# A fused four-layer decoder: wide attention's first maxima and last exponentials for two heads at once, and the feedforward's products behind the maxima of layer 2

## The reference, cut to what matters

```python
# layer 2, both attentions: 16 heads of width 8, softmax over 256 keys
# layer 2, feedforward (batches one by one)
h = layernorm(x, ln1_w, ln1_b); h = bitlinear(h, w1, b1)     # 128 -> 512, int8 activations, ternary weights
h = gelu(h); h = layernorm(h, ln2_w, ln2_b); x = x + bitlinear(h, w2, b2)
# layer 3, self-attention ("wide": 16 heads of width 64)
q, k, v = x @ Wq + bq, x @ Wk + bk, x @ Wv + bv
prob = softmax(k_h . q_h / 8);  out = sum(prob * v);  x = x + concat(out) @ Wo + bo
# layer 3, attention between the 16 heads of one token ("cross" below)
energy = einsum('nhld,ngld->nlhg', q, k); attn = softmax(energy / sqrt(128), axis=3)
out = layernorm(einsum('nlhg,ngld->nhld', attn, v)); x = x + out @ Wo.T + bo
# then layer 3's feedforward, which needs all batches
```

## Time and profile before

| | us |
|---|---|
| time, median of 3 runs | 1146.28 (1145.36 to 1150.3) |
| the profiled execution: device time | 1154.05 |
| the profiled execution: span from first to last instruction | 1152.2 |
| PE busy in the span | 854.2 (74%) |
| DVE busy | 605.4 (53%) |
| ACT busy | 358.4 (31%) |
| POOL busy | 317.2 (28%) |
| mean granted clock of PE | 0.849 |

### The profile page before, as it was taken

How to read it: one execution, slowest core, us unless ns; L and a number is a source line. 1 busy time by engine, 2 the same in 40 slices (tenths; PEclk the granted TensorE clock), 3 DMA queues, 4 the chain that set the end, 5 groups by cost and what they waited for, 6 DMA issues and landing times. The chain is left out here.

```text
span 1152.2 us, 16025 instructions
## 1 busy us (share of the span) xinstructions
PE 854.2 (74%) x5977; PEld 613.6 (53%) x5977; DVE 605.4 (53%) x1422; ACT 358.4 (31%) x697; POOL 317.2 (28%) x319
## 2 busy tenths in 40 slices
PE   5965887854676175688776757999999997367984
PEld 2532454553343173567653335576877775244884
DVE  2655852314499933585666886435236456642222
ACT  1110574220121112055544633453432332111331
POOL 1353100212168704132221111000034343415222
PEclk9975898985678597599988878899999997658998
DMA  9302200540000007053561000000000000005674
GB/s 374 118 1 81 69 5 1 164 131 7 19 0 1 0 1 165 10 116 65 139 179 52 3 1 0 1 2 2 2 1 2 1 2 1 0 1 189 194 262 154
DMA packets 44678, 72.44 MB, mean 63 GB/s; under 512 B 4817, under 2 KB 36737, under 8 KB 43033
## 3 DMA queue, kind: packets, MB, share of 16 engines
q1 hardware_dynamic: 38921, 65.72, 19.4%
q0 software_dynamic: 1728, 3.59, 0.9%
q10 hardware_dynamic: 3952, 2.10, 0.7%
HBM read 58.65 MB, written 15.89 MB: 65 GB/s over the span
## 5 line engine op out<-in xcount | busy, mean ns | idle before, releaser
L848 DVE TENSOR_REDUCE space<-PS 128x2 f32<-128x512 f32 x128 | 83.5, 686 | 42.6 <-PE PS L652 42.1
L2517 DVE TENSOR_REDUCE space<-PS 128x2 f32<-128x512 f32 x64 | 44.3, 692 | 114.3 <-PE PS L2221 114.3
L832 ACT ACTIVATE annex<-PS 128x384 f32<-128x384 f32 (+1 forms) x128 | 67.4, 545 | 59.7 <-PE PS L663 30.2
L2237 PE MATMUL PS<-space 64*128 64x256 f32 x256 | 80.4, 407 | 0.0
L2256 PEld LDWEIGHTS PS<-space 128*128 128x128 f32 x512 | 62.4, 192 | 23.0 <-issue 19.4
L2256 PE MATMUL PS<-space 128*128 128x65 f32 x512 | 71.1, 282 | 2.6 <-ACT space L2344 2.6
L1951 POOL TENSOR_TENSOR space<-space 128x1536 f32<-128x1536 f32 x16 | 54.6, 3439 | 39.1 <-ACT space L1824 32.9
L1171 PE MATMUL PS<-space 128*128 128x128 f32 x444 | 55.6, 278 | 9.3 <-DVE space L1306 5.4
L2344 ACT ACTIVATE space<-PS 128x512 f32<-128x512 f32 x64 | 38.2, 597 | 74.1 <-PE PS L2238 74.1
L1171 PEld LDWEIGHTS PS<-space 128*128 128x128 f32 x444 | 51.7, 192 | 12.3 <-DVE space L1306 6.5
L1306 DVE TENSOR_TENSOR space<-PS,space 128x512 f32<-128x512 f32 (+1 forms) x28 | 19.2, 687 | 71.6 <-ACT space L1233 66.4
(11 more groups left out here) (494 smaller groups left out, 2259.8 us busy)
## 6 DMA issues: line engine op xcount, KB each, us to landing
space<-in_e_l_ffn SPq DMA_DIRECT2D x22, 768.0 KB
space<-in_e_l_ffn SPq DMA_DIRECT2D x23, 192.0 KB, 2.7
l_ffn_sorted<-in_slots SPq DMA_DIRECT2D x2, 1584.0 KB, 25.9
space<-l_attn_scratch_k SPq DMA_DIRECT2D x8, 384.0 KB
space<-l_ffn_sorted SPq DMA_DIRECT2D x10, 264.0 KB, 4.4
weights<-in_w_l_xattn SPq DMA_DIRECT2D x1, 2504.0 KB, 15.3
weights<-in_w_l_attn SPq DMA_DIRECT2D x1, 2124.0 KB, 12.1
space<-l_xattn_scratch_q SPq DMA_DIRECT2D x4, 512.0 KB, 3.5
```

The costliest lines, as they stand in the source:

```text
L832: nc.scalar.activation(P[:, u % 8, 0:keys], PS[:, 3 + u % 2, 0:keys], ACT.Exp).then_inc(exp_done, 1)
L848: nc.vector.tensor_reduce(m[:, :, at_h], max_bank(u).rearrange("p (c k) -> p c k", c=2), AX_X, ALU.max).then_inc(max_done, 1)
L2237: nc.tensor.matmul(out, kk[:, 128 * kc:128 * kc + 128], q, start=True, stop=False)
L2517: nc.vector.tensor_reduce(MX[:, half % 2, :, h], PS[:, a % 2, :].rearrange("p (c k) -> p c k", c=2), AX_X, ALU.max).then_inc(max_done, 1)
```

## The change

1. **Two heads at once.** The first 16 units have their first products in pairs, two units a step (program steps 176 to 183), interleaved half by half; after that one a step. The second product of unit i stands 9 steps behind the wide step 0 instead of 13, one a step up to unit 46 (ALONE = 47); the last 17 units have theirs in pairs, in 9 steps. Third products and DVE's normalisations follow one and two steps behind. The maxima of the first 16 units use four banks (0, 1, 3, 4), the exponentials of the last 17 units the same four. P, the buffer of exponentials, has 4 slots instead of 3.
2. **Later start.** SHIFT goes from 163 to 176. The wide units run in program steps 176 to 241 instead of 163 to 240.
3. **The feedforward by a table.** The steps of its chain are written out per batch (PLAN). No job of it stands before program step 133: `banks_at` gives no bank there. Layer 2's maxima keep three banks to their end, where the last 16 units had two. Batches 2 and 3 come later relative to the rest: f3 of batch 1 stands at program step 172 (160 before), quant2 of batch 2 at 184 (166 before), f4 of batch 3 at 204 (190 before).
4. **f1 and f3 leave PSUM by DVE** instead of ACT.
5. **The cross attention** keeps its own offsets, but starts 4 steps behind the last second product of its batch. For batch 2 that is program step 243 (234 before) with its products at 249 (238 before), because banks 0, 1, 3 and 4 are in use by exponentials up to step 240. For batch 3 the products stand at 255 (254 before).

```diff
-WIDE_LAG = 13
-SHIFT = 163
+SHIFT = 176
...
-        return PS[:, u % 3 if mqa or u < U - 16 else (u + 1) % 2, :]
+        return PS[:, u % 3, :]
...
+    PLAN = {"in": (-58, -42, -24, -9), "twice": (-54, -38, -20, -6), "norm1": (-50, -34, -16, -2), "quant1": (-49, -33, -11, -1),
...
+    LEAD, DELAY, ALONE = HEADS // 2, 9, 47
+
+    def first_at(a):
+        return a // 2 if a < HEADS else a - LEAD
+
+    def second_at(i):
+        return i + DELAY if i < ALONE else ALONE + DELAY + (i - ALONE) // 2
...
+    max_bank = [(0, 1, 3, 4)[a % 4] if a < HEADS else a % 2 for a in range(UNITS)]
+    exp_bank = [3 + i % 2 if i < ALONE else (0, 1, 3, 4)[(i - ALONE) % 4] for i in range(UNITS)]
...
     def banks_at(step):
-        return (2,) if step + shift < before.last_max + 2 else (2, 1) if step < -4 else (2, 3) if step < 12 else (7, 2)
+        return () if step + shift < before.last_max + 2 else (2, 1) if step < -1 else (7, 2)
...
-            place(16 * b + 8 * half + 10, "M", b, half)
+            place(first_at(16 * b + 8 * half + 7) + 3, "M", b, half)
         for i in range(6):
-            place(16 * b + 32 + i + i // 3, ("t", "t", "o")[i % 3], b, i)
+            place(second_at(16 * b + 15) + 4 + i + i // 3, ("t", "t", "o")[i % 3], b, i)
...
+            for qc in range(2):
+                for a in units:
+                    b, r, g, q, kk = half_of(a)
+                    last = nc.tensor.matmul(PS[:, max_bank[a], 256 * qc:256 * qc + 256], q[:, 128 * qc:128 * qc + 128], kk, start=True, stop=True)
...
             for kc in range(2):
+                for i in units:
+                    b, r, g, q, kk = half_of(i)
+                    out = PS[:, exp_bank[i], 256 * kc:256 * kc + 256]
+                    nc.tensor.matmul(out, kk[:, 128 * kc:128 * kc + 128], q, start=True, stop=False)
+                    last = nc.tensor.matmul(out, c.ones3[r:r + 64, :], MTR[r:r + 64, b % 2, g, :], start=False, stop=True)
...
-            if kind == "f1":
-                ins = nc.scalar.copy(QF[:, b % 2, 0, 0:256], out[:, 0:128].bitcast(BF16))
-            elif kind == "f3":
-                ins = nc.scalar.copy(QF[:, b % 2].rearrange("p t f -> p (t f)"), out.bitcast(BF16))
...
+            elif kind == "f1":
+                nc.vector.tensor_copy(QF[:, b % 2, 0, 0:256], out[:, 0:128].bitcast(BF16)).then_inc(free[bank_of[i]], 1)
+            elif kind == "f3":
+                nc.vector.tensor_copy(QF[:, b % 2].rearrange("p t f -> p (t f)"), out.bitcast(BF16)).then_inc(free[bank_of[i]], 1)
```

More of the change, by code:

```diff
@@ L2109, in released @@
     def released(where):
-        return {1: (before.max_done, before.units), 2: (before.max_done, before.units - 17), 3: (before.exp_done, before.units),
-                7: before.free[1]}[where]
+        return {1: (before.max_done, before.units), 2: (before.max_done, before.units), 7: before.free[1]}[where]
     seq = before.sequence
```

178 lines of the change are left out of this document (92 added, 86 removed), and 3 rows, old and new, of the table PLAN.

## The result

The changed kernel takes 1137.57 us (median of 20 runs), beside 1148.19 us for the kernel before on the same chip. The ratio is 0.9916, with a 95% interval of 0.989 to 0.9942: 9.6 us faster (6.7 to 12.6). The prediction said 1132.3 us, 1119 to 1146, and faster. Of the 14 us that it expected to gain, 9.6 came.

What follows compares the result with a forecast made beforehand. Bounds by stage: DVE nearly up to 642.7 us, feedforward chain to 698.8, PE from 744.4 to 963.8, no engine in the tail. Terms 0 - 29 + 15 = -14 took the median from 1146.28 to 1132.3 us, range 1119 to 1146.

Steps and rivals of the forecast that it cites:

- the two large terms: First pair to last third product, -29 us (-16 to -34), and the tail behind it, +15 us (+9 to +22).
- the first term: Layer 2's last maxima and DVE's chain up to the first pair: 0 us, between -6 and +10.
- the second: From the first pair to the last third product: 236 instead of 265.0 us, -29, between -16 and -34.
- I allow 5 us of waits: DVE's chain behind layer 2's last maximum: 46 us of work plus 5 us of waits, T at 691.2.
- f3's copy: DVE's copy of f3 out of PSUM before the first pair: 1.2 us each for two, bounds 0.69 and 1.4.
- The first stage: Up to layer 2's last maxima: 2.5 us less, at least 0, at most 6.
- unit 19's first product: Sign of being right in the wide units: unit 19's first product near 726, first pair near 699.
- DVE is the limit: New lead, up to unit 19: DVE needs 27.4 us against 26 of PE's own work.
- 2 us of waits and 2 at half clock: PE in the new lead: 2 us of waits and 2 at half clock, within 13 for the stage.
- a gap of over 3 us from 726 on: Sign of being wrong: gaps of PE over 3 us between 726 and 935.
- The tail: From the last third product to the cross attention's last addition: 67.6 instead of 52.6 us, +15, between +9 and +22.
- only then shift's exponential, since ACT's queue has it behind xq's copy: Tail: ACT runs the exponential only after batch 3's xk, xv, xT, xq and copies, 6.2 us; the exponential takes 0.7.

Runs made afterwards that it cites:

- e5: Changed kernel with batch 0's f1 and the weights' sums one program step earlier, 132 instead of 133; ratio to the kernel before 0.9871.
- e9: Changed kernel with f1 one step early and norm2 of batch 0 four program steps earlier, ahead of L890; ratio to the kernel before 0.9872.
- e1: Changed kernel with both first products of each lead pair reading the same 64 rows of the array; ratio to the kernel before 0.9908.
- e2: Changed kernel with both second products of each pair from unit 47 on reading the array's upper 64 rows; ratio to the kernel before 0.9978.
- e4: Changed kernel with the copies of f1 and f3 out of PSUM back on ACT; ratio to the kernel before 0.9858.
- e8: Changed kernel with cross attention of batches 2 and 3 reordered: sums three steps later, exponential one step earlier; ratio to the kernel before 0.9797.
- e7: Changed kernel with shift and exponential of batches 2 and 3 in the cross attention three steps earlier; ratio to the kernel before 0.9863.
- e11: Changed kernel without any pairs, second products 13 steps behind the first, one a step to the end; ratio to the kernel before 0.98.
- e6: Changed kernel with batch 0's attn, normed and T ahead of batch 1's quant2, batch 1's f3 and f4 later; ratio to the kernel before 0.9933.
- c1: Changed kernel run again unaltered; ratio to the kernel before 0.9912.
- e3: Changed kernel without pairs among the last second products (ALONE = 64), the lead still paired; ratio to the kernel before 0.988.
- e10: Changed kernel with f1 and f3 copies on ACT, front order and tail order together; median 1126.7 us, ratio to the kernel before 0.9792.

## Why the prediction was right, and where its steps were not

The time, the sign and the two large terms came out: 1137.57 for 1132.3, -33.4 for -29 and +15.9 for +15 us. The gain of the three stages was 10.5 us and not 14, and it owes something to luck: the first term missed by 7.0 us one way, the second by 4.4 the other. The steps:

*Up to the first pair: 0 predicted, +7.0 measured* (-3.2 and +10.2), inside the bounds of -6 and +10. This is the mis-sized term, and its step is "I allow 5 us of waits". The work was right: DVE is busy 44.0 of the 57.8 us from the last maximum to T, 46 predicted. It stood without work for 13.8 us, not 5. e5 and e9 show why: DVE passes L890 about 21.7 us behind the last maximum whatever it does before, since layer 2's units that this addition needs have to pass PE, ACT and DVE first, and it has less than that to do (13.2 us in the changed kernel; behind L890 it is busy 30.5 of 35.6 us). I treated all of DVE's work as one pile behind the last maximum; it is two, and only the one behind L890 counts. f3's copy took 0.68 and 0.66 us, and not my 1.2, which made up for 1 us. The prediction's estimate from the Trainium skill, "VectorE: DVE Perf Modes" (at most twice the basic rate out of PSUM by the section "The perf-mode tier table", in the cycles of the errata section), had been 0.66, and the trace agrees with it. The first stage gained 3.2 us, 2.5 predicted: PE's wait for the maxima fell from 7.7 to 4.2 us.

*From the first pair to the last third product: -29 predicted, -33.4 measured.* PE's own work can be had from the windows, as the stage less the time in which PE stood still and less what the clock took (its shortfall from 1.00 times the window). Before: 265.0 - 14.1 - 13.1 = 237.8 us. After: 231.6 - 8.6 - 8.7 = 214.3. So work fell by 23.5 (21 predicted: 14 by pairs, 7 by jobs that now come later), and waits and clock together from 27.2 to 17.3. I had 21 to 13 there: my sums of work, 244 and 223, were 6 and 9 us too high, and the waits too low by as much. Pairs cost 1.07 and 1.29 us (1.0 and 1.33 predicted), and e1 and e2 show that they cost 1.92 and 2.37 within one half. Within the stage a mark was missed: unit 19's first product comes at 741.93, 37.3 us behind the first pair, where I had 27, and the rest takes 194.4 us instead of 209. "DVE is the limit" in the lead held, but I gave it "2 us of waits and 2 at half clock"; it was 4.2 of waits, and 5.8 us of clock between 730.93 and 745 alone. With the copies on ACT (e4) unit 19 is 27.8 us behind the first pair. PE's wait of 3.30 us that ended at 725.99 also comes near what the prediction named as a sign of being wrong, a gap of over 3 us from 726 on.

*The tail: +15 predicted, +15.9 measured.* 14.1 us to batch 2's products (14.9), 54.4 from there (52.7 in the value taken). The step "only then shift's exponential, since ACT's queue has it behind xq's copy" is the 5.85 us wait, and e8 takes it away. What I missed is that the wait's obvious remedy fails (e7).

*What no step of the prediction said* is that the pairs were not needed. e11 does the same work as the kernel before (241.2 - 4.1 = 237.1 us against 237.8) and gains 23.8 us in this stage with no pair, 10.0 of them from waits and 13.1 from the clock. 16.5 of the 23.8 us lie in the lead (45.6 us before, 29.1 in e11). There the kernel before had batch 2's f3 and f4 among its first units (those of batches 0 and 1 stood ahead of the first unit in both kernels). Its PE in order of time:

```profile
712.59 0.82 PE L2150 MATMUL PS<-small_tile,const_tile 128*128 128x128 bf16 x8 [4.37 <-DVE const_tile L2383]
...
723.68 1.03 PE L2155 MATMUL PS<-const_tile 128*128 128x128 bf16 x8
...
729.54 1.76 PE L2166 MATMUL PS<-XT,weights 128*128 128x256 f32 x4 [1.96 <-DVE X L2503]
```

f3 waits 4.37 us for quant2, a projection behind f4 waits 1.96 us for attn: these two are all that PE stood still in this lead, and the clock is at half from about 712.8 to 726.5 and again from 730 to 733. In e11 batch 2's f3 comes at the lead's end, without a wait:

```profile
733.91 0.61 PE L2164 MATMUL PS<-small_tile,const_tile 128*128 128x128 bf16 x8
```

That this is the cause was not tried alone (e11 keeps the third bank, the copies on DVE and the fourth buffer), but e6, which puts batch 1's f4 and attn among the first units, lengthens the lead by 5.8 us. The pairs then take 15 us and the jobs behind the stage 8 us out of it, and give back 4.5 in waits, 8.7 in clock and 16 in the tail: 6.4 us lost in all. The prediction credited the pairs with 14 of its 29 us and booked the tail's 15 apart; it did not see these two as one exchange. The 10 us lost before the first product have nothing to do with pairs (e11: 66.2 us too, against 56.1). So of the 23.8 us that e11 gains behind it, 13.8 are left in the sum of the distances (359.9 against 373.7).

Left open: why the clock fell in e4 at about 750.3, where PE had waited at most 1.22 us at a time, while waits of 1.22 us at 759.48 in the changed kernel and of 1.21 us at 737.02 in e11 were followed by no fall; why the tail is 1.6 us longer in e1, e2 and e6; and how e11 would do with the orders of e8 and e9. This was not run. e8's gain, at least, is not there to be won: ahead of dens e11 waits 1.10 and 0.69 us, not 5.85. The 4.3 us in layer 3 were not looked into beyond seeing the same 23.01 MB of transfers, at 175 instead of 169 GB/s.

## What to carry to other kernels

Two products in different halves of PE's rows took one product's time here (1.07 us, and 1.92 within one half), but that is only a gain where nothing else paces the stage: count what the engine behind needs per pair, and look at the granted clock behind every wait that this brings. Work that no longer stood among the units that wait for it went with 24 us less behind the first product and 10 more ahead of it, and the pairs on top, with their shorter distance, cost 6. Ahead of a cut in work on one engine, ask where in its queue the next instruction stands that waits for someone else: what was cut before it brought nothing here (e5, 4.8 us of waiting).

## What the runs showed of the hardware

*A DVE instruction held by POOL.* Besides e7, the changed kernel has three such places. DVE and POOL in order of time, one of them:

```profile
844.42 3.60 DVE L2552 TENSOR_SCALAR space<-space 128x16 bf16<-128x16 f32 x1
848.05 0.18 DVE L2554 SCALAR_TENSOR_TENSOR space<-space 128x16 f32<-128x16 f32 x1
```

```profile
839.02 8.96 POOL L2608 TENSOR_TENSOR weights<-CTX,annex 128x2048 f32<-128x2048 f32 x2 [8.60 <-ACT space L2323]
```

L2552 takes 0.17 us where POOL is idle (724.93). Here it ends 0.04 us behind POOL's product (847.98), and so at 872.09 (3.06 us) and 902.91 (2.67). Reductions and products with an operand in PSUM ran beside POOL's products at their usual length (2.29 us for L2504 and 2.23 for L2475 in the tail, both under POOL's 5.43). The Trainium skill, "SBUF — State Buffer", section "SBUF: two separate sides", says that VectorE and GpSimd share a pair of SBUF ports, locked for a whole instruction by whichever comes first, and that VectorE asks for it in its two-port fast modes and, against a GpSimd operation that reads SBUF, with two SBUF inputs. The trace agrees for these TENSOR_SCALARs, each of which started while POOL's product ran; in which mode they run it does not show, and for two SBUF inputs it has no row.

*The clock.* In the kernel without pairs (e11) it stayed at 1.00 between 705 and 946 us. In the changed kernel it was at half from about 725.3 to 742.4, and it fell 2.6 us into a wait of 3.30 us; the seven other kernels with the same lead (c1, e2, e3, e5, e7, e8, e9) show the same 17 us behind the same wait. In the kernel before it fell at about 712.8, behind a wait of 4.37 us. In e4 and e10 it fell some 2 us behind the end of a wait of 1.22 us and stayed at half for 20.5 us, longer than in the others.
